# A hand-ordered cross-attention and FFN kernel: the FFN's second half runs one pair later, and the order of every engine is rewritten

## The chip, the cores and the metric

The kernel runs on one core of a Trainium2 chip. The metric is the device time in microseconds (us) from start to end of one launch; three runs of the kernel before gave 957.84, 962.15 and 962.29, median 962.15. The engines are named as in the profile: PE is TensorE (matrix products), PEld its weight loads, DVE is VectorE, ACT is ScalarE, POOL is GpSimd, SP is the engine that issues most DMAs. All of them work through their own list of instructions strictly in order and meet only at semaphores.

## The reference

32 batches of 56 queries attend with 16 heads (head size 8) to 1500 context rows each; then comes a feed-forward net with ternary weights and 8-bit activations.

```
x = x + xattn(layernorm(x), ctx, ctx, mask)      # q,k,v projections with bias, 16 heads,
                                                 # softmax(where(mask==0, -1e9, q.k/sqrt(8))) @ v, Wo, bo
x = x + ffn(layernorm(x))                        # gelu(bitlinear(x,w1)) -> bitlinear(.,w2)
bitlinear(x,w): round(x*127/max|x|) clipped, times ternary w (by mean |w|)
```

## The kernel before

The 32 batches go through one software pipeline. A step is one batch; steps come in pairs (even, odd), and `steps` runs `first_even`, `first_odd`, then a loop over 14 pairs of `even` and `odd`, then `last_even`, `last_odd`, and at last `tail`. What an engine does in a step is a written list of words, and all engines' lists have to agree on the order in which PSUM banks are filled. The words and what they do:

- `T0..T2` (PE transposes of the context, L741; ACT copies them out to `ctx_t`, L621), `K0..K2` (key projection, L744; ACT writes `k_full` by `kf`, L641, then `k_hi` by `kh`, L651; POOL writes `k_lo` by `kl`, L573), `V0..V2` (value projection, L748; ACT copies, L631). T and K are for the batch two ahead, V for the next.
- `sum` (ACT, L611: whether a query has any key) then `some` (DVE), `F0` (PE, L751; DVE writes `q_flag`), `q` (POOL: `q_hi`, `q_lo`, `qry_hi`, `qry_lo`, L562 to L566).
- `M0..M11` (PE, L803): products of next batch's queries with keys, only for the row maxima. Each is two products of 64 rows and 500 columns, each in a bank of its own; DVE takes each with `m` (L1091). `neg0`, `R0` turn the maxima into `shift`, which a DMA puts into `own_query`.
- `S0..S11` (PE, L820; `s0 f0` is S0 in two parts): this batch's scores, per chunk of 125 keys four products (hi/hi, hi/lo, lo/hi and the mask bias), each as two 64-row products side by side; ACT takes the two banks of a chunk with `e` (L659, exponential).
- `P0..P2` (PE, L856): probabilities times values, in tiles of 32 columns, for four chunks each. `own0`, `D0` (denominators, L772) and `O0` (output projection, L768) follow; O0 is done once for a pair of batches, and DVE adds it to `x_rows` (L1066).
- The output chain of a pair after that: `rows0` (layer norm statistics, 14 dependent small DVE operations from L900 on), `rows1` (normalise and quantise, L952 to L962), `H0` (PE transposes the rows, L777), `G0` (first FFN product, L779; ACT applies gelu, L628), `hid0..hid3` (DVE quantises the hidden layer, L982 to L992), `U0` (PE transposes it, L782), `Y0` (second product, L786; DVE adds to `x_rows`, L1078), and a DMA stores the rows.

M and S products use half of PE's rows each, side by side (64 rows); the others use the full array (P: tiles of 32 columns).

PSUM has one bank for P and seven (`NBANK`) for all else. A slot is a bank's turn; slots go round in PE's written order, S and M taking two each. So a slot can be filled only when the slot seven places earlier has been read out:

```
bank = {s: (n - len(slots)) % NBANK for n, s in enumerate(slots)}
```

`wait_bank_free` makes PE wait for that reader, `wait_bank_full` the reader for PE. The line with `left_bank` says which semaphore a reader moves. ACT holds one function table at a time: gelu needs another than exp, and a load of a table stands in its list where a function is not in the present one.

Of the kernel before, what the change touches and what calls it, by code (L numbers as in the profile page):

```python
# [126 lines left out]
def passes(open_, lead, even, odd, tail, more_even, more_odd):  # L127

    return {"open": order(open_), "lead": order(lead), "first_even": with_more(even, more_even, ahead=(0, 1, 2)),
            "first_odd": with_more(odd, more_odd), "even": even, "odd": odd,  # L130
            "last_even": ahead_only(even, (-1, 0, 1)), "last_odd": ahead_only(odd, (-1, 0)), "tail": order(tail)}
# [1048 lines left out]
```

How the kernel before makes its waits and increments, by code:

```python
        def wait(e, semaphore, value):  # L360
            if not isinstance(value, int) or value > 0:
                e.wait_ge(semaphore, value)
# [28 lines left out]
        def wait_bank_free(e, slot, how, st):  # L392
            last, ago = before(how, slot)
            if last is not None:
                e.wait_ge(left_bank[last[0]], number(last, later(st, -ago)))
# [1 line left out]
        def wait_bank_full(e, slot, how, st):  # L397
            k = BANK[how][slot]
            e.wait_ge(bank_full[k], fills_before(how, st[1], k) + signalled(how, k).index(slot) + 1)
# [34 lines left out]
            def place_shift(bt):  # L434
                b, k, p = bt
                sp.wait_ge(shift_ready, b + 1)
                for h in range(2):
                    row = SLOT * h + SQ
                    sp.dma_start(own_query[row:row + 1, p, :, :].bitcast(F32),
                                 shift[4 * h:4 * (h + 1), :, 0:SQ].bitcast(F32)).then_inc(shift_placed[p], 16)
# [1 line left out]
            def store(bt):  # L443
                t, rows = pair_of(bt), PAIR * D
                at, added = t * rows, t + 1
                if not isinstance(t, int):
                    at, added = sp.snap(at), sp.snap(added)
                sp.wait_ge(out_ready, added)
                src = x_flat[:, bass.ds(t * D if isinstance(t, int) else sp.snap(t * D), D)]
                sp.dma_start(out_flat[bass.ds(at, rows)].rearrange("(r d) -> r d", d=D), src).then_inc(stored, 16)
# [124 lines left out]
            def fold_bias():  # L576
                pool.wait_ge(xn_ready, NGRP)
                pool.wait_ge(bo_folded, 1)
```

## Time and profile before

| | |
|---|---|
| runs | 957.84, 962.15, 962.29 us |
| the profiled execution | 959.75 us, span from first to last instruction 958.0 us |
| PE busy | 887.8 us, 93% of the span |
| DVE busy | 753.1 us, 79% |
| ACT busy | 673.4 us, 70% |
| POOL busy | 231.5 us, 24% |
| mean granted PE clock | 0.976 of full |
| one loop iteration (two batches) | 54.17 us |

A busy share is an average over the span; PE's ends are modelled, so that two products that overlap in the pipeline both count. The distance between the starts of two products is the better measure of what PE pays. A row of a timeline has the start in us, its length, the engine, the line, the operation, what it writes and reads, how many instructions are merged, and in brackets the idle time ahead of it with what ended it.

### The profile page before, as it was taken

To read this page: it belongs to the slowest core of one execution; us is meant where nothing else is said; L and a number is where in the kernel's file an instruction comes from. 1 tells how busy PE (TensorE), PEld (TensorE's weight loads), DVE (VectorE), ACT (ScalarE), POOL (GpSimd) and SP (SyncE) were. 2 spreads that over 40 slices of the span, in tenths; PEclk is the share of its full clock that TensorE was granted. 3 is DMA by queue.
4 is the path that set the end of the run, shared out by engine and by line. 5 is a ranking of instruction groups with operands and counts; after the bars stand their busy time and mean duration, and the time that the engine had idled before them with its cause. 6 is when DMAs were issued, how large, how long until landed. Compare 5 with 4: busy or idle time off the path is not lost.

```text
span 958.0 us, 33628 instructions
## 1 busy us (share of the span) xinstructions
PE 887.8 (93%) x11716; PEld 694.2 (72%) x11716; DVE 753.1 (79%) x2593; ACT 673.4 (70%) x1272; POOL 231.5 (24%) x253
## 2 busy tenths in 40 slices
PE   3767989999999999999999999999999999999983
PEld 2344767777787787778787777777787777778772
DVE  3687568888788878888788888888787888888744
ACT  2543667777887877777886777777887777777661
POOL 6310142230222222130222222131222222031200
PEclk9788999999999999999999999999999999999997
DMA  5520221122222211122222211122222111220000
GB/s 130 127 62 1 63 61 29 42 57 60 63 60 63 59 34 47 46 60 60 63 60 63 53 32 50 51 60 60 63 60 61 49 32 50 56 60 0 4 2 6
DMA packets 59375, 49.34 MB, mean 52 GB/s; under 512 B 2785, under 2 KB 55633, under 8 KB 59345
## 3 DMA queue, kind: packets, MB, share of 16 engines
q1 hardware_dynamic: 57551, 48.11, 19.0%
q10 hardware_dynamic: 1793, 0.83, 0.4%
q8 instruction: 18, 0.29, 0.1%
q14 instruction: 13, 0.10, 0.0%
HBM read 47.91 MB, written 0.92 MB: 51 GB/s over the span
## 4 chain that ended last, share of the span: by engine, by line
issue 66%; POOL 18%; PE 7%; DVE 5%; ACT 1%; DMA 1%; POOLq 1%; DVEq 0%; ACTq 0%
POOL k_lo L573 8%; POOL qry_hi L565 4%; POOL qry_lo L566 4%; PE ps_p L820 2%; DMA ctx_sb<-in_ctx_dram 1%; PE ps_p L803 1%; DVE max_junk L1091 1%; POOL q_lo L563 1%; POOL q_hi L562 1%; PE ps_v L856 1%; PE ps_p L744 1%; ACT probs L659 1%; POOL x_rows L581 0%; PE ps_p L741 0%; POOLq L556 0%
## 5 line engine op out<-in xcount | busy, mean ns | idle before, releaser
L1091 DVE CUSTOM_DVE_ANT_0 max_junk<-ps_p,mask_bias 120x500 bf16<-120x500 f32 x768 | 481.6, 675 | 125.3 <-PE ps_p L803 104.5
L659 ACT ACTIVATE probs<-ps_p 125x448 f32<-125x448 f32 x768 | 359.3, 551 | 87.0 <-PE ps_p L820 81.6
L573 POOL TENSOR_TENSOR k_lo<-k_full,k_hi 128x500 fp32r<-128x500 f32 x96 | 119.8, 1262 | 592.0 <-ACT k_hi L651 587.2
L856 PE MATMUL ps_v<-probs,vals 125*32 125x112 f32 x6144 | 162.9, 262 | 0.8 <-issue 0.4
L803 PE MATMUL ps_p<-k_hi,qry_hi 64*120 64x500 f32 x768 | 148.8, 413 | 15.6 <-POOL qry_hi L565 6.5
L820 PE MATMUL ps_p<-qry_hi,k_hi 64*125 64x448 f32 x768 | 158.6, 403 | 4.4 <-DVE seg_max L1091 1.7
L856 PEld LDWEIGHTS ps_v<-probs,vals 125*32 125x32 f32 x6144 | 146.9, 111 | 21.1 <-issue 17.7
L641 ACT ACTIVATE k_full<-ps_p,bk_sb 128x500 f32<-128x500 f32 x96 | 64.7, 674 | 123.1 <-PE ps_p L744 122.6
L820 PE MATMUL ps_p<-own_query,mask_bias 57*125 57x448 f32 x768 | 145.7, 368 | 0.0
L820 PE MATMUL ps_p<-qry_lo,k_hi 64*125 64x448 f32 x768 | 144.4, 366 | 0.0
L820 PE MATMUL ps_p<-qry_hi,k_lo 64*125 64x448 f32 x768 | 144.3, 365 | 0.0
L803 PEld LDWEIGHTS ps_p<-k_hi,qry_hi 64*120 64x120 f32 x768 | 71.5, 181 | 51.7 <-issue 22.4
L820 PEld LDWEIGHTS ps_p<-qry_hi,k_hi 64*125 64x125 f32 x768 | 74.7, 185 | 47.0 <-ACT probs L659 17.4
L744 PE MATMUL ps_p<-ctx_t,wk_sb 128*128 128x500 f32 x192 | 100.8, 620 | 4.1 <-DVE seg_max L1091 4.0
L748 PE MATMUL ps_p<-wv_sb,ctx_t 128*125 128x128 f32 x768 | 100.9, 278 | 0.7 <-DVE seg_max L1091 0.7
L748 PEld LDWEIGHTS ps_p<-wv_sb,ctx_t 128*125 128x125 f32 x768 | 90.1, 188 | 10.3 <-issue 9.0
L820 PEld LDWEIGHTS ps_p<-own_query,mask_bias 57*125 57x125 f32 x768 | 75.0, 184 | 5.2 <-DMA own_query<-shift 0.4
L820 PEld LDWEIGHTS ps_p<-qry_lo,k_hi 64*125 64x125 f32 x768 | 74.9, 185 | 5.2
L820 PEld LDWEIGHTS ps_p<-qry_hi,k_lo 64*125 64x125 f32 x768 | 75.4, 186 | 4.1
L741 PE MATMUL ps_p<-ident,ctx_sb 125*128 125x125 f32 x384 | 57.7, 282 | 13.8 <-DMA ctx_sb<-in_ctx_dram 13.8
L631 ACT ACTIVATE vals<-ps_p 125x512 f32<-125x512 f32 x96 | 55.6, 597 | 18.8 <-PE ps_p L748 17.1
L1091 DVE DVE_READ_ACCUMULATOR2_ANT seg_max<- 120x1 f32 x768 | 63.8, 83 | 0.0
(124 smaller groups left out, 831.5 us busy)
## 6 DMA issues: line engine op xcount, KB each, us to landing
ctx_sb<-in_ctx_dram SPq DMA_DIRECT2D x31, 750.0 KB
mask_sb<-in_mask_Bx1xSxS_ik_dram SPq DMA_DIRECT2D x64, 328.1 KB
own_query<-shift SPq DMA_DIRECT2D x64, 1.8 KB
out_dram<-x_rows SPq DMA_DIRECT2D x16, 56.0 KB, 1.6
ctx_sb<-in_ctx_dram ACTq DMA_DIRECT2D x1, 750.0 KB
x_rows<-in_x_dram SPq DMA_DIRECT2D x1, 672.0 KB, 10.9
w_sb<-in_L_ffn_w_dram SPq DMA_DIRECT2D x2, 256.0 KB, 8.8
x_rows<-in_x_dram SPq DMA_DIRECT2D x1, 224.0 KB, 5.9
```

The source lines that it names most:

```text
L565: put_q(pool.tensor_tensor(qry_hi[:, p, :, 0:SQ], head_of_row[:], heads_of(q_hi[:]), ALU.mult))
L573: pool.tensor_tensor(k_lo[:, p, at], k_full[:, (p + n) % 2, :], k_hi[:, p, at].bitcast(F32), ALU.subtract)\
L631: act.activation(vals[:, p, 4 * n:4 * n + 4, :, 0, :].rearrange("p c v r -> p (c v) r"), bank[0:KC, :].rearrange("p (v r) -> p v r", r=VH) ...
L641: act.activation(k_full[:, (p + n) % 2, :], ps_p[:, BANK[how]["K", n, 0], 0:SEG], ACT.Identity, bias=bk_sb[:, 0:1]).then_inc(k_full_ready, 1)
L659: act.activation(probs[:, c % NP, h], ps_p[0:KC, BANK[how]["S", c, h], 0:HC], ACT.Exp)\
L741: mm = pe.transpose(bank[:, c * KC:(c + 1) * KC], ctx_sb[:, p, 4 * n + c, :], ident[0:KC, 0:KC])
L744: mm = pe.matmul(bank[:, 0:SEG], wk_sb[:], ctx_t[:, p, n * SEG:(n + 1) * SEG], start=True, stop=True)
L748: mm = pe.matmul(bank[0:KC, c * D:(c + 1) * D], ctx_t[:, p, at:at + KC], wv_sb[:], start=True, stop=True)
L803: pe.matmul(ps_p[0:MROWS, BANK[how]["M", n, h], 0:SEG], qry_hi[rows, p, 2 * r:2 * r + 2, :].rearrange("p a q -> p (a q)")[:, 0:MROWS], k_h ...
L820: mm = pe.matmul(ps_p[0:KC, BANK[how]["S", c, h], 0:HC].rearrange("k (a q) -> k a q", a=HH), key[part, :], query[part], start=(n == 0), st ...
L856: mm = pe.matmul(ps_v[r:r + VT, col:col + PAIR], vals[:, p, c, t].rearrange("p a r -> p (a r)"), src, start=(c == 0 and t < 4), stop=(c == ...
L1091: dve.tensor_tensor_reduce(max_junk[0:MROWS, BANK[how][slot], :], ps_p[0:MROWS, BANK[how][slot], 0:SEG], mask_bias[0:MROWS, p, s * SEG:(s ...
```

## The change

`U`, `Y` and `hid` get a lag of two pairs instead of one (`PAIR_LAG`): a pair's `rows`, `H0`, `G0` still run in the same pair of steps, while `hid0..hid3`, `U0` and `Y0` run in the even step after. Since the second pair of steps has no such work yet, it becomes a variant of its own (`early_even`, `early_odd`), the loop has 13 iterations instead of 14, and the one tail becomes three (`tail_even`, `tail_odd`, `tail_last`), with one more store at the end.

```
+PAIR_LAG = {"U": 2, "Y": 2, "hid": 2}
...
-        def pair_of(st):
-            return st[1] - 1
+        def pair_of(st, kind=""):
+            return st[1] - PAIR_LAG.get(kind, 1)
...
-            with e.Fori(1, B // 2 - 1) as i:
+            step(batch(1, 0), "early_even")
+            step(batch(1, 1), "early_odd")
+            with e.Fori(2, B // 2 - 1) as i:
...
-    PE_EVEN, PE_ODD, "D0 O0 H0 G0 U0 Y0",
+    PE_EVEN, PE_ODD, ("D0 U0 O0 Y0", "H0 G0", "U0 Y0"),
...
-    DVE_EVEN, DVE_ODD, "own D0 O0 rows0 rows1 H0 hid0 hid1 hid2 hid3 U0 Y0",
+    DVE_EVEN, DVE_ODD, ("hid0 own D0 hid1 hid2 hid3 U0 O0 rows0 rows1 Y0", "H0", "hid0 hid1 hid2 hid3 U0 Y0"),
...
-                if p == 1 and (loop or b > 1):
+                if p == 1 and (loop or b > 3):
                     store(bt)
...
+            store(batch(B // 2 + 1, 1))
```

All lists of the two loop steps are new. In PE's, the stretches of full-array words between M and S words become fewer and longer; the four even and odd lists of PE and ACT are:

```
before, PE even: T0 T1 V0 M0 s0 f0 M1 S1 S2 M2 S3 M3 S4 S5 M4 S6 S7 M5 M6 P0 D0 K0 M7 S8 S9 M8 S10 M9 O0 S11 M10 M11
                 T2 K1 F0 V1 V2 K2 R0 P1 P2
before, PE odd:  V0 T0 H0 s0 M0 f0 S1 S2 M1 S3 S4 M2 M3 G0 P0 M4 S5 M5 S6 S7 M6 S8 S9 M7 S10 S11 M8 M9 P1 P2 M10 M11
                 K0 U0 V1 T1 Y0 T2 D0 K1 F0 K2 R0 V2
after, PE even:  T0 V0 K0 T1 M0 s0 f0 S1 M1 S2 M2 S3 S4 M3 S5 M4 S6 S7 M5 S8 M6 M7 P0 P1 M8 S9 M9 S10 S11 M10 M11
                 D0 V1 U0 T2 V2 F0 K1 O0 P2 K2 Y0 R0
after, PE odd:   T0 V0 T1 T2 K0 H0 M0 s0 f0 M1 S1 S2 M2 S3 S4 M3 S5 S6 M4 S7 S8 M5 S9 M6 S10 S11 M7 M8
                 K1 V1 V2 K2 G0 M9 M10 M11 P0 P1 P2 F0 R0 D0
before, ACT odd: sum0 V0 T0 e0 ... e9 G0 e10 ... e23 kf0 kh0 T1 V1 T2 kf1 kh1 kf2 V2 kh2
after, ACT odd:  T0 V0 T1 T2 kf0 e0 ... e21 kh0 e22 e23 kf1 V1 V2 kf2 sum0 kh1 kh2 G0
```

On ACT, the head of the even step in the kernel before (`ctx_t` is a T word, `vals` a V word, `probs` an exponential; ISA and REGISTER_ALU rows are waits and their registers):

```order
L621 ACTIVATE ctx_t<-ps_p 128x500
L399 ISA
L621 ACTIVATE ctx_t<-ps_p 128x500
L363 ISA
L631 ACTIVATE vals<-ps_p 125x32x16
L363 ISA
L658 ISA
L659 ACTIVATE probs<-ps_p 125x448 x2
L658 REGISTER_ALU
L659 ACTIVATE probs<-ps_p 125x448 x2
```

The same place on ACT in the changed kernel, behind the first `ctx_t` (`mask_sum_junk` is the word `sum0`, `k_full` is `kf0`); the row that follows is the first exponential:

```order
L623 ACTIVATE mask_sum_junk,mask_sum<-mask_sb 56x1500
L406 ISA
L370 ISA
L653 ACTIVATE k_full<-ps_p,bk_sb 128x500
L406 ISA
L370 ISA
L643 ACTIVATE vals<-ps_p 125x32x16
L406 ISA
L633 ACTIVATE ctx_t<-ps_p 128x500
L370 ISA
L670 ISA
L671 ACT_TABLE_LOAD
```

The mask sum and `k_full` have moved ahead of the first exponential, and the load of the exp table, which stood behind gelu in the middle of the odd step's exponentials, now stands between the last copy and the first exponential of the even step.

On PE, the way from the even step's `R0` to the odd step's `H0` (`w_sb` into `ident_bf`, 128x112) in the kernel before:

```order
L753 MATMUL ps_p<-ident,neg_max 8x120
L856 MATMUL ps_v<-probs,vals 32x112 x32
L850 ISA
L856 MATMUL ps_v<-probs,vals 32x112 x32
L748 MATMUL ps_p<-wv_sb,ctx_t 125x128 x4
L741 MATMUL ps_p<-ident,ctx_sb 128x125 x4
L777 MATMUL ps_p<-ident_bf,w_sb 128x112
```

And in the changed kernel from the second row behind O0 (`wo_rows,attn`) on, which now stands in this same stretch, to H0:

```order
L870 MATMUL ps_v<-probs,vals 32x112 x32
L747 REGISTER_ALU
L758 MATMUL ps_p<-ctx_t,wk_sb 128x500
L800 MATMUL ps_p<-w2t,w_sb 112x128 x4
L767 MATMUL ps_p<-ident,neg_max 8x120
L755 MATMUL ps_p<-ident,ctx_sb 128x125 x4
L762 MATMUL ps_p<-wv_sb,ctx_t 125x128 x4
L755 MATMUL ps_p<-ident,ctx_sb 128x125 x8
L747 ISA
L758 MATMUL ps_p<-ctx_t,wk_sb 128x500
L791 MATMUL ps_p<-ident_bf,w_sb 128x112
```

O0 stood between M and S words before, with two S and M words, nine full-array words and both P words between it and H0; now P2, K2, Y0, R0 and five T, V, K words lie between.

## Rows read from the trace of the kernel before

**Rows 1.** One loop iteration; busy us and instructions by engine, then clock, DMA:
```profile
400.77:454.94 54.17, 53.48 (x733) 42.34 (x732) 45.06 (x156) 41.77 (x80) 13.24 (x15) 1.00 0.20 54
```
**Rows 2.** Timeline of PE, even step, second half:
```profile
421.28 0.40 PE L803 MATMUL ps_p<-k_hi,qry_hi 64*120 64x500 f32 x2
421.61 0.69 PE L768 MATMUL ps_p<-wo_rows,attn 128*112 128x128 f32 x4
422.23 0.47 PE L820 MATMUL ps_p<-qry_hi,k_hi 64*125 64x448 f32 x2
422.53 0.36 PE L820 MATMUL ps_p<-qry_hi,k_lo 64*125 64x448 f32 x2
...
423.15 0.61 PE L803 MATMUL ps_p<-k_hi,qry_hi 64*120 64x500 f32 x4
423.70 0.65 PE L741 MATMUL ps_p<-ident,ctx_sb 125*128 125x125 f32 x4
424.18 1.01 PE L744 MATMUL ps_p<-ctx_t,wk_sb 128*128 128x500 f32 x2
...
425.05 1.99 PE L748 MATMUL ps_p<-wv_sb,ctx_t 128*125 128x128 f32 x16
426.88 1.00 PE L744 MATMUL ps_p<-ctx_t,wk_sb 128*128 128x500 f32 x2
...
427.92 3.27 PE L856 MATMUL ps_v<-probs,vals 125*32 125x112 f32 x128
...
432.97 0.22 PE L777 MATMUL ps_p<-ident_bf,w_sb 112*128 112x112 bf16 x1 [0.28 <-DVE w_sb L962]
```
**Rows 3.** Timeline of PE, even step's M0:
```profile
406.56 0.48 PE L803 MATMUL ps_p<-k_hi,qry_hi 64*120 64x500 f32 x2 [0.25 <-issue]
```
**Rows 4.** Timeline of ACT, the even step's end and the odd step:
```profile
429.96 1.45 ACT L611 ACTIVATE mask_sum_junk<-mask_sb 56x1500 bf16<-56x1500 int32 x1
...
432.37 0.60 ACT L631 ACTIVATE vals<-ps_p 125x512 f32<-125x512 f32 x1 [0.88 <-PE ps_p L748]
432.87 0.58 ACT L621 ACTIVATE ctx_t<-ps_p 128x500 f32<-128x500 f32 x1
...
440.55 0.69 ACT L628 ACTIVATE wtern<-ps_p,row_stat 112x512 f32<-112x512 f32 x1
441.26 1.28 ACT L659 ACT_TABLE_LOAD   x1
442.55 6.49 ACT L659 ACTIVATE probs<-ps_p 125x448 f32<-125x448 f32 x14
```
**Rows 5.** The page's groups, ACT's k_full:
```profile
L641 ACT ACTIVATE k_full<-ps_p,bk_sb 128x500 f32<-128x500 f32 x96 | 64.7, 674 | 123.1 <-PE ps_p L744 122.6
```
**Rows 6.** Timeline of PE in the odd step, scores beside gelu:
```profile
442.71 0.36 PE L820 MATMUL ps_p<-own_query,mask_bias 57*125 57x448 f32 x2
443.15 0.47 PE L820 MATMUL ps_p<-qry_hi,k_hi 64*125 64x448 f32 x2
```
**Rows 7.** Timeline of DVE, from O0's sum to rows1's last:
```profile
423.06 0.29 DVE L1066 TENSOR_TENSOR x_rows<-ps_p,x_rows 112x128 f32 x1
...
426.55 0.28 DVE L900 BATCH_NORM_STATS2 row_stat<-x_rows 112x6 f32 x1
...
430.28 1.03 DVE L952 TENSOR_SCALAR w_sb<-x_rows,row_stat 112x128 f32 x1
...
432.68 0.23 DVE L962 TENSOR_SCALAR w_sb<-w_sb 112x128 bf16<-112x128 f32 x1
```
**Rows 8.** Timeline of POOL, first odd step:
```profile
126.21 4.71 POOL L581 TENSOR_TENSOR x_rows<-x_rows,bo_sb 112x2048 f32<-112x2048 f32 x1
```
**Rows 9.** Timeline of PE, the loop's first M0:
```profile
133.21 0.48 PE L803 MATMUL ps_p<-k_hi,qry_hi 64*120 64x500 f32 x2 [2.88 <-POOL qry_hi L565]
```
**Rows 10.** A window behind that wait, columns as in rows 1:
```profile
134.70:138.10 3.40, 3.40 (x20) 2.99 (x20) 1.67 (x6) 2.05 (x5) 1.97 (x2) 0.50 0.62 166
```
**Rows 11.** Timeline of PE, H0 of the last pair of steps:
```profile
918.96 0.22 PE L777 MATMUL ps_p<-ident_bf,w_sb 112*128 112x112 bf16 x1 [1.93 <-DVE w_sb L962]
```

More of the change, by code:

```diff
@@ L64 @@
 PE_EVEN = order("""
-    T0 T1 V0 M0 s0 f0 M1 S1 S2 M2 S3 M3 S4 S5 M4 S6 S7 M5 M6 P0 D0 K0 M7 S8 S9 M8 S10 M9 O0 S11 M10 M11 T2 K1 F0
-    V1 V2 K2 R0 P1 P2
+    T0 V0 K0 T1 M0 s0 f0 S1 M1 S2 M2 S3 S4 M3 S5 M4 S6 S7 M5 S8 M6 M7 P0 P1 M8 S9 M9 S10 S11 M10 M11 D0 V1 U0 T2
+    V2 F0 K1 O0 P2 K2 Y0 R0
 """)
 ACT_EVEN = order("""
-    T0 T1 V0 e0 e1 e2 e3 e4 e5 e6 e7 e8 e9 e10 e11 e12 e13 e14 e15 sum0 kf0 e16 e17 e18 e19 e20 e21 e22 kh0 e23
-    T2 kf1 kh1 kf2 V1 V2 kh2
+    T0 sum0 kf0 V0 T1 e0 e1 e2 e3 e4 e5 e6 e7 e8 e9 e10 e11 e12 e13 e14 e15 e16 e17 e18 e19 e20 e21 e22 e23 kh0
+    kf1 T2 V1 V2 kh1 kf2 kh2
 """)
 DVE_EVEN = order("""
-    own0 m0 m1 m2 m3 m4 m5 m6 m7 m8 m9 bias0 m10 m11 m12 m13 D0 m14 m15 m16 m17 m18 m19 O0 some0 bias1 m20 m21
-    m22 m23 F0 neg0 rows0 R0 rows1 bias2
+    own0 hid0 m0 m1 m2 m3 m4 m5 hid1 m6 m7 m8 m9 some0 m10 hid2 m11 m12 m13 m14 bias0 hid3 m15 m16 m17 m18 m19
+    m20 m21 m22 m23 D0 U0 O0 neg0 F0 rows0 Y0 R0 rows1 bias1 bias2
 """)
@@ L87 @@
 PE_ODD = order("""
-    V0 T0 H0 s0 M0 f0 S1 S2 M1 S3 S4 M2 M3 G0 P0 M4 S5 M5 S6 S7 M6 S8 S9 M7 S10 S11 M8 M9 P1 P2 M10 M11 K0 U0 V1
-    T1 Y0 T2 D0 K1 F0 K2 R0 V2
+    T0 V0 T1 T2 K0 H0 M0 s0 f0 M1 S1 S2 M2 S3 S4 M3 S5 S6 M4 S7 S8 M5 S9 M6 S10 S11 M7 M8 K1 V1 V2 K2 G0 M9 M10
+    M11 P0 P1 P2 F0 R0 D0
 """)
 ACT_ODD = order("""
-    sum0 V0 T0 e0 e1 e2 e3 e4 e5 e6 e7 e8 e9 G0 e10 e11 e12 e13 e14 e15 e16 e17 e18 e19 e20 e21 e22 e23 kf0 kh0
-    T1 V1 T2 kf1 kh1 kf2 V2 kh2
+    T0 V0 T1 T2 kf0 e0 e1 e2 e3 e4 e5 e6 e7 e8 e9 e10 e11 e12 e13 e14 e15 e16 e17 e18 e19 e20 e21 kh0 e22 e23
+    kf1 V1 V2 kf2 sum0 kh1 kh2 G0
 """)
 DVE_ODD = order("""
-    H0 own0 m0 m1 m2 m3 m4 m5 m6 m7 m8 m9 m10 m11 hid0 m12 m13 bias0 m14 m15 hid1 m16 some0 hid2 hid3 m17 bias1
-    m18 m19 m20 m21 U0 m22 m23 neg0 Y0 bias2 D0 R0 F0
+    H0 m0 m1 m2 m3 m4 m5 m6 m7 m8 m9 bias0 m10 m11 m12 m13 m14 m15 own0 m16 m17 m18 m19 m20 some0 m21 m22 m23
+    neg0 bias1 R0 F0 D0 bias2
 """)
 POOL_ODD = order("""
-    kl0 q0 kl1 kl2
+    kl0 kl1 kl2 q0
 """)
@@ L129, in passes @@
     return {"open": order(open_), "lead": order(lead), "first_even": with_more(even, more_even, ahead=(0, 1, 2)),
[L130 to L131 removed]
+            "first_odd": with_more(odd, more_odd), "early_even": [s for s in even if s[0] not in PAIR_LAG],
+            "early_odd": odd, "even": even, "odd": odd,
+            "last_even": ahead_only(even, (-1, 0, 1)), "last_odd": ahead_only(odd, (-1, 0)),
+            "tail_even": order(tail[0]), "tail_odd": order(tail[1]), "tail_last": order(tail[2])}
 PE_PASS = passes(
@@ L182, in fills_before @@
 def fills_before(how, i, bank):
-    first = sum(len(signalled(h, bank)) for h in ("open", "lead", "first_even", "first_odd"))
+    first = sum(len(signalled(h, bank)) for h in ORDER[:ORDER.index(None)])
     body = len(signalled("even", bank)) + len(signalled("odd", bank))
     if how in ("even", "odd"):
-        return first + (i - 1) * body + (len(signalled("even", bank)) if how == "odd" else 0)
-    order = ["open", "lead", "first_even", "first_odd", None, "last_even", "last_odd", "tail"]
-    return sum((B // 2 - 2) * body if h is None else len(signalled(h, bank)) for h in order[:order.index(how)])
+        return first + (i - 2) * body + (len(signalled("even", bank)) if how == "odd" else 0)
+    return sum((B // 2 - 3) * body if h is None else len(signalled(h, bank)) for h in ORDER[:ORDER.index(how)])
 def before(how, slot):
@@ L199, in before @@
         return None, 0
-    there = PREVIOUS[how]
-    return [s for s in FLAT[there] if BANK[there][s] == bank][-1], 1
+    there, ago = PREVIOUS[how], 1
+    while not any(BANK[there][s] == bank for s in FLAT[there]):
+        there, ago = PREVIOUS[there], ago + 1
+    return [s for s in FLAT[there] if BANK[there][s] == bank][-1], ago
 def xattn_ffn(nc, x, ctx_in, mask, wq, bq, wk, bk, wv, bv, wo, bo, w1, w2, out):
```

37 lines of the change are left out of this document (24 added, 13 removed).

## The prediction

> **What bounds the kernel now.** I read the page's shares first, then the windows of single loop iterations, then PE's timeline through one iteration, and last the timelines of ACT and DVE at the places where PE's products are further apart than usual. An iteration (one pair of batches) takes 54.17 us, and PE is busy for 53.48 of it at full clock, with DVE at 45.06 and ACT at 41.77 [rows 1]. So PE is the path, and the sum is made on PE: what it pays for crossing between kinds of product, and where it waits in its written order. The chain of waits is of little use here (it follows POOL); distances between the starts of PE's products tell more.
>
> A crossing is seen in rows 2. Two maxima pairs and the way out of them to T0 take 0.55 us (423.15 to 423.70), one pair and the way out to O0 0.33 (421.28 to 421.61): so a pair costs 0.22 and the way out 0.11. Behind O0 the first score product holds PE for 0.30 (422.23 to 422.53), where the ones after it are some 0.20 apart: 0.1 for coming back, beside a way out of O0 that I price like the way in, 0.11. That is the price that the change attacks.
>
> **Crossings.** I count in the two lists. Before, an iteration has six stretches of full-array words between M and S words, which makes 12 crossings, and inside them 4 more between P (tiles of 32 columns) and full-array words; after, four stretches with 8, and 3 inside. 5 crossings fewer by 0.11 are 0.55 us, and two returns to M and S fewer by 0.1 are 0.2: -0.75 us an iteration. Bounds: 0 if crossings hide behind weight loads in the new places, -1.5 if each costs twice as much. I take -0.75, since rows 2 show it at two places.
> The Trainium skill has a rule for this (TensorEngine Tiling (Array Packing), Key Properties: a change of tiling mode drains TensorE, a change of tile alone does not). The trace agrees that something of this kind is paid, with 0.11 us a time; by that rule alone the kernel would get faster, which is the first rival below.
>
> **Waits that go.** M0 of the even step waits 0.25 us before and starts with a refill [rows 3]; it is held by POOL's qry_hi, which needs F0. In the new lists F0 stands ahead of R0, D0, T0, V0, K0, T1, some 3 us before M0 and about as long as the chain of q_flag, q_hi, q_lo and qry_hi; -0.3. Gelu with its two table loads no longer stands among the odd step's exponentials: there a score product came 0.44 behind its forerunner instead of 0.20 and the next paid the refill [rows 6]; -0.35.
>
> **The head of the even step: a wait that comes.** This is the largest term. ACT's list there is now T0, sum0, kf0, V0, T1, table load, e0. Let PE start T0 at 0. T0's copy can start at about 0.75 (0.65 of products [rows 2] and a hand-over of 0.1) and the next ACT instruction 0.5 later (432.37 to 432.87 [rows 4]), at 1.25. The mask sum takes 1.45 and a little for reading the sum: 2.8. k_full 0.67 [rows 5]: 3.45. V0 0.5: 3.95. T1 0.58: 4.55. The table load is 1.28, and no gap stands on either side of it (gelu ends at 441.24, load 441.26 to 442.54, exponential 442.55 [rows 4]): 5.83. e0, 0.55, ends at 6.4.
> PE in the same time: T0 0.48, V0 0.91, K0 0.84, T1 0.48 [rows 2] make 2.7; M0 with its way in 0.33, S0 0.9, S1 0.8, M1 0.2: it wants S2 at 4.95. But S2 takes the slots seven behind M0's second and S0's first, so it waits for e0, until about 6.45: 1.5 us. It restarts with a refill of 0.1. The exponentials then come 0.46 apart (6.49 less 0.55, by 13 [rows 4]); S3 needs e3, at 7.8, where PE would be ready at 7.5: 0.3 more. After that ACT has caught up, because two scores and a maximum (1.85 on PE) give it as long as its four exponentials need. Together +1.95 us. ACT reaches this place in time otherwise: in the odd step's end P0, P1, P2 give it 4.8 us (1.6 each by 3.27 for two [rows 2]) for sum0, kh1, kh2, the gelu table and gelu, so F0, which needs gelu's bank, does not wait. Bounds: 0 (if S2 is not held) and +2.6 (if ACT comes 0.6 late).
> On the table the Trainium skill says more than the trace (ScalarE: Activation LUTs, What ACT_TABLE_LOAD costs: 1283 ns for the load and some 1380 ns of drain at every switch). By that page the term would be an estimated 1.4 us larger in each of 13 iterations, 18 us in all. The trace agrees on the load and shows no drain (0.02 us on one side, 0.01 on the other [rows 4]), so the sum goes without it.
>
> **H0: a wait that grows.** Before, O0 stood in the even step's S and M words; DVE had its sum at 423.06, and H0 still waited for rows1 to end [rows 2, 7]. The bracket says 0.28, from T0's start I make it 0.44. Now O0 stands behind K1, and the chain from O0 to H0 is shorter on PE than on DVE. DVE: O0's products and hand-over 0.75, its sum 0.3, neg0 and F0 0.2, from the first of rows0 to rows1's first 3.73 [rows 7] with the 0.23 of waiting in it out and Y0's sum (0.27) in: 3.77; rows1 from 430.28 to 432.91, 2.63; 0.05 to PE. That is 7.7. PE from O0: O0 0.55, P2 1.65, K2 0.95, Y0 and R0 0.35, T, T, T 1.35, V0 0.9, K0 0.85, in all 6.6. H0 waits 1.1 to 1.2, against 0.44: +0.75. Nothing hides it: behind H0 on PE stand M0 and all scores of the odd step, and ACT and DVE are idle until then. Bounds: 0 (rows1's first, 1.03 us here, has the shape of operations that take 0.3 us) and +1.3.
>
> **Other edits.** hid0 to hid3 and U0, Y0 are the same work in another step; DVE has 9 us free in an iteration [rows 1], and in the even step they lie beside the new wait of S2: nothing. The store waits for a Y0 that is now done a step earlier: nothing, and place_shift, behind it in SP's queue, is not held. q0 behind kl1 and kl2 on POOL: both end before q_flag is there.
>
> **Once only.** At the first loop iteration PE waits 2.88 us for POOL [rows 9], because bias folding (4.71 us [rows 8]) stands between kl0 and q0 and kl0 came late; 1.5 us after it the granted clock is 0.50, 1.2 GHz, for 3.4 us [rows 10], in which half, 1.7, is lost. In the new list kh0 comes before e22, so kl0 and the folding start earlier and run beside P0 to P2: -4.6. Bounds 0 and -4.6. The last pair and the tail: H0 waits 1.93 already [rows 11] and will wait some 1.5 more, gelu no longer splits the last scores (-1.5), and the tail has one more hid and U0 ahead of O0 (+1.5 to +3): together +1, bounds -2 and +5. The second pair has no table load at its head; I count it as 0.
>
> **The sum.** -0.75 - 0.3 - 0.35 + 1.95 + 0.75 = +1.3 us an iteration, by 13 iterations +17; -4.6 + 1 for what is once only: +13.3. The profiled execution took 959.75 (span 958.0): 973. The median of the runs is 962.15, 2.4 above it, so between 973 and 975.5; I say 974, 1.2% slower.
>
> **Rivals.**
> Fewer crossings win (ends on the other side). If PE's S2 is not held at the even head (ACT arrives at e0 before PE has S0 and M1 behind it) and H0's wait stays as it was, then -1.4 by 13, -4.6, +1: about 938. It decides as soon as the head's wait is under 0.65 with H0's +0.75, or under 1.4 without it. For: crossings and the M0 wait are plain in the rows, and ACT is only 77% busy in an iteration. Against: four ACT operations and a load stand in writing between T0 and e0, and their durations are measured; only PE being later than I think helps. Chance 0.2.
> They cancel. Half the head's wait (0.95) and half of H0's growth (0.4): -0.05 an iteration; with the once-only part 956 to 962. For: both are differences of sums of ten terms each. Chance 0.13.
> The clock falls. The wait of 2.88 was followed by 3.4 us at 1.2 GHz [rows 9, 10]; if the new waits of 1.5 and 1.2 us do the same once in each iteration, 1.7 us by 13 come on top: 996. For: such waits now come in every iteration. Against: they are half as long, with a busy PE on both sides. Chance 0.1.
> The forecast has the remaining 0.57, with a range of its own of 964 to 985.
>
> A difference under 0.5% (about 4.8 us) is what a measurement of this kernel cannot tell from none. Faster by more: the first rival, 0.2. Within: the second, and the forecast's low edge, 0.14. Slower: 0.66. The range, 950 to 990, leaves out the lower part of the first rival and the clock.
>
> **What would show it.** In the changed kernel's PE timeline: a gap of about 1.5 us ahead of the score chunk that follows the even step's M1, ended by ACT's probs; a table load directly ahead of e0, with ACT busy from T0's copy up to it; H0's idle at 1.1 us, released by rows1's last; the iteration's length at 55.5; no wait for POOL at the loop's first M0. Wrong would be: an iteration under 54, or e0 starting less than 0.5 us behind the end of S0.

## The result

The changed kernel takes 980.57 us (median of four runs, 978.93 to 983.31), the kernel before 961.01 in the same session: the ratio is 1.0211, with a 95% interval of 1.0175 to 1.0247. The forecast was 974, slower by 1.2%; it is slower by 2.1%. The profiled execution took 983.31 us, its span 981.6, against 958.0 before: 23.6 us more. The medians differ by 19.6; the profiled execution is the slowest of the changed kernel's four, and its start is part of why (see "Once only").

I put the 23.6 on the places of the trace by the distances between H0 (one in each pair of steps from the second on). The first H0 is at 161.37 before and at 157.57 after: -3.8. From there to that of the last pair of steps (rows 11 before, 942.59 after) are 14 distances, 757.6 us before and 785.0 after: +27.4, or 1.96 each. From that H0 to the end are 39.1 us before and 39.0 after. A loop iteration, which took 54.17 us [rows 1], now takes 56.16. A window of one iteration of the changed kernel: us, then busy us and instructions of PE, PEld, DVE, ACT and POOL, then clock and DMA:

```profile
494.70:550.86 56.16, 53.76 (x730) 42.66 (x731) 46.80 (x156) 41.78 (x79) 13.28 (x14) 1.00 0.19 52
```

PE has nearly the same busy time (53.48 before) at full clock; 1.7 of the 2 us are idle time. PE's timeline shows two places where most of it lies. The even step's head (answers to rows 3):

```profile
517.12 0.20 PE L765 MATMUL ps_p<-some_diag,ones_bf 128*128 128x56 bf16 x1
517.29 0.26 PE L767 MATMUL ps_p<-ident,neg_max 120*8 120x120 f32 x1
517.51 0.47 PE L786 MATMUL ps_p<-pv_own,den_of_row 128*128 128x112 f32 x2
518.10 0.64 PE L755 MATMUL ps_p<-ident,ctx_sb 125*128 125x125 f32 x4
...
520.95 0.49 PE L817 MATMUL ps_p<-k_hi,qry_hi 64*120 64x500 f32 x2
...
522.91 0.39 PE L817 MATMUL ps_p<-k_hi,qry_hi 64*120 64x500 f32 x2
524.26 0.47 PE L834 MATMUL ps_p<-qry_hi,k_hi 64*125 64x448 f32 x2 [0.96 <-ACT probs L671]
...
525.18 0.45 PE L817 MATMUL ps_p<-k_hi,qry_hi 64*120 64x500 f32 x2
525.65 0.47 PE L834 MATMUL ps_p<-qry_hi,k_hi 64*125 64x448 f32 x2
```

M0 (520.95) no longer waits. Behind M1 (522.91) the chunk S2 starts 1.35 us later, where a maxima pair needs 0.20; behind M2 the chunk S3 starts 0.47 later. ACT in the same stretch (answers to rows 4):

```profile
514.29 1.28 ACT L640 ACT_TABLE_LOAD   x1
515.58 0.69 ACT L640 ACTIVATE wtern<-ps_p,row_stat 112x512 f32<-112x512 f32 x1
518.78 0.59 ACT L633 ACTIVATE ctx_t<-ps_p 128x500 f32<-128x500 f32 x1 [2.50 <-PE ps_p L755]
519.26 1.44 ACT L623 ACTIVATE mask_sum_junk<-mask_sb 56x1500 bf16<-56x1500 int32 x1
520.60 0.19 ACT L623 ACTIVATION_READ_ACCUMULATOR mask_sum_junk<-mask_sb 56x1 f32 x1
520.71 0.68 ACT L653 ACTIVATE k_full<-ps_p,bk_sb 128x500 f32<-128x500 f32 x1
521.29 0.59 ACT L643 ACTIVATE vals<-ps_p 125x512 f32<-125x512 f32 x1
521.76 0.59 ACT L633 ACTIVATE ctx_t<-ps_p 128x500 f32<-128x500 f32 x1
522.37 1.28 ACT L671 ACT_TABLE_LOAD   x1
523.67 2.73 ACT L671 ACTIVATE probs<-ps_p 125x448 f32<-125x448 f32 x6
```

From T0's copy (518.78) to the first exponential ACT has no pause; before that it stands idle for 2.50 us with gelu's table in it. The forecast had put S2 at 6.45 us behind T0's start; it is 6.16 (518.10 to 524.26).

The second place is H0, first on PE (answers to the end of rows 2), then the chain on DVE (answers to rows 7):

```profile
542.97 0.66 PE L782 MATMUL ps_p<-wo_rows,attn 128*112 128x128 f32 x4
...
548.66 1.01 PE L758 MATMUL ps_p<-ctx_t,wk_sb 128*128 128x500 f32 x2
550.86 0.22 PE L791 MATMUL ps_p<-ident_bf,w_sb 112*128 112x112 bf16 x1 [1.19 <-DVE w_sb L978]
```

```profile
543.78 0.29 DVE L1082 TENSOR_TENSOR x_rows<-ps_p,x_rows 112x128 f32 x1 [0.66 <-PE ps_p L782]
...
548.37 0.83 DVE L968 TENSOR_SCALAR w_sb<-x_rows,row_stat 112x128 f32 x1
...
550.58 0.23 DVE L978 TENSOR_SCALAR w_sb<-w_sb 112x128 bf16<-112x128 f32 x1
```

From O0's start to H0's are 7.89 us, set by O0's products and DVE's chain behind them; the forecast had 7.7.

**Where an iteration's time goes.** For each word of PE I take the distance to the next word's start, less what such a word takes where nothing is in its way (a maxima pair 0.20, a transpose 0.11 and so on). What is left over in an iteration, mean of six iterations, in us:

| | before | after | difference | forecast |
|---|---|---|---|---|
| ways between M/S, full-array and P words (16, then 11) | 1.97 | 1.54 | -0.43 | -0.55 |
| the refill behind such a way | 1.15 | 0.89 | -0.26 | -0.20 |
| M0's wait | 0.30 | 0 | -0.30 | -0.30 |
| gelu's table among the scores | 0.34 | 0 | -0.34 | -0.35 |
| head of the even step (M1 to S2, M2 to S3, two refills) | 0 | 1.61 | +1.61 | +1.95 |
| H0 | 0.45 | 1.34 | +0.89 | +0.75 |
| small waits inside M/S stretches | 1.20 | 1.52 | +0.32 | 0 |
| small waits inside full-array stretches | 0.25 | 0.71 | +0.46 | 0 |
| in none of these lines | 0 | 0.04 | +0.04 | 0 |
| sum | 5.66 | 7.65 | +1.99 | +1.30 |

### The profile page after: what moved, and what is told of

Read it like the earlier page. It is cut to its first block, busy times and chain, and to the rows that moved or that the text cites. A ratio compares the mean times of both kernels' runs of the same rounds, so it can differ in the third digit from the quotient of the medians.

```text
span 981.6 us, 33626 instructions
## 1 busy us (share of the span) xinstructions
PE 890.9 (91%) x11716; PEld 700.3 (71%) x11716; DVE 776.2 (79%) x2593; ACT 670.4 (68%) x1270; POOL 232.2 (24%) x253
## 4 chain that ended last, share of the span: by engine, by line
issue 60%; POOL 16%; PE 15%; DVE 6%; DMA 1%; ACT 1%; POOLq 1%; DVEq 0%; ACTq 0%
POOL k_lo L585 8%; PE ps_p L834 6%; POOL qry_hi L577 3%; POOL qry_lo L578 3%; PE ps_v L870 2%; PE ps_p L817 2%; PE ps_p L758 1%; DMA ctx_sb<-in_ctx_dram 1%; DVE max_junk L1107 1%; PE ps_p L762 1%; POOL q_lo L575 1%; POOL q_hi L574 1%; PE ps_p L755 1%; POOLq L568 0%; DVE ps_p L1068 0%
## 5 line engine op out<-in xcount | busy, mean ns | idle before, releaser
L834 PE MATMUL ps_p<-qry_hi,k_hi 64*125 64x448 f32 x768 | 156.3, 395 | 13.4 <-ACT probs L671 12.7
L817 PE MATMUL ps_p<-k_hi,qry_hi 64*120 64x500 f32 x768 | 157.9, 424 | 9.3 <-DVE seg_max L1107 4.5
L870 PE MATMUL ps_v<-probs,vals 125*32 125x112 f32 x6144 | 158.0, 260 | 0.4 <-issue 0.2
L758 PE MATMUL ps_p<-ctx_t,wk_sb 128*128 128x500 f32 x192 | 104.7, 630 | 2.6 <-DVE seg_max L1107 2.6
L762 PEld LDWEIGHTS ps_p<-wv_sb,ctx_t 128*125 128x125 f32 x768 | 92.1, 190 | 9.2 <-ACT probs L671 7.6
L633 ACT ACTIVATE ctx_t<-ps_p 128x500 f32<-128x500 f32 x96 | 54.1, 584 | 45.6 <-PE ps_p L755 45.6
```

Source lines behind the costliest of these rows:

```text
L633: act.activation(ctx_t[:, p, n * SEG:(n + 1) * SEG], bank[:, 0:SEG], ACT.Copy)\
L758: mm = pe.matmul(bank[:, 0:SEG], wk_sb[:], ctx_t[:, p, n * SEG:(n + 1) * SEG], start=True, stop=True)
L762: mm = pe.matmul(bank[0:KC, c * D:(c + 1) * D], ctx_t[:, p, at:at + KC], wv_sb[:], start=True, stop=True)
L817: pe.matmul(ps_p[0:MROWS, BANK[how]["M", n, h], 0:SEG], qry_hi[rows, p, 2 * r:2 * r + 2, :].rearrange("p a q -> p (a q)")[:, 0:MROWS], k_h ...
L834: mm = pe.matmul(ps_p[0:KC, BANK[how]["S", c, h], 0:HC].rearrange("k (a q) -> k a q", a=HH), key[part, :], query[part], start=(n == 0), st ...
L870: mm = pe.matmul(ps_v[r:r + VT, col:col + PAIR], vals[:, p, c, t].rearrange("p a r -> p (a r)"), src, start=(c == 0 and t < 4), stop=(c == ...
```

## The experiments

The length of an iteration (mean of nine) is the measure; it is free of what differs at the start from run to run. The changed kernel has 56.16, before 54.17. A time without a ratio is that of a single run.

**The table load ahead of its wait.** A one-column exponential behind gelu brings exp's table back at once:

```
                     act.activation(... gelu ...)
+                    wait(act, table_back, pair_of(st))
+                    act.activation(table_junk[:], bk_sb[:], ACT.Exp).then_inc(table_back, 1)
```

> The changed kernel with one more tiny exponential (128x1, into a scratch tile) right behind gelu on ACT, so that the exp table is loaded there, in ACT's 2.5 us of idle time ahead of T0, and not ahead of e0. Theory: e0 starts 1.3 us earlier, the gap M1 to S2 shrinks from 1.35 us to some 0.3, M2 to S3 from 0.47 to 0.22: -1.4 us an iteration, 14 times, about 961 to 963. Rival (the mask sum and k_full hold ACT anyway): under -0.5 an iteration, above 973.

Measured: 965.94, ratio 1.0058 (1.003 to 1.0086), iteration 55.05. That is 1.11 an iteration less, where 1.4 was expected. The leftover at S2 falls from 1.15 to 0.27 and that at S3 disappears. ACT's timeline:

```profile
504.67 0.69 ACT L642 ACTIVATE wtern<-ps_p,row_stat 112x512 f32<-112x512 f32 x1
505.37 1.28 ACT L644 ACT_TABLE_LOAD   x1
506.67 0.20 ACT L644 ACTIVATE table_junk<-bk_sb 128x1 f32<-128x1 f32 x1
507.85 0.59 ACT L635 ACTIVATE ctx_t<-ps_p 128x500 f32<-128x500 f32 x1 [0.98 <-PE ps_p L759]
```

The load now stands in what was ACT's idle time. This is the cause of 1.1 of the 1.6 us at the head. The Trainium skill (ScalarE: Activation LUTs, What ACT_TABLE_LOAD costs) counts 1283 ns of load and about 1380 ns of drain at a switch. The load of 1.28 us is here; no drain shows at either load, also not between two of them (0.01 to 0.02 us around each).

**The mask sum out of the head.** `sum0` moves behind e17, DVE's `some0` behind m15:

```
-    T0 sum0 kf0 V0 T1 e0 ... e17 e18
+    T0 kf0 V0 T1 e0 ... e17 sum0 e18
```

> The changed kernel with ACT's mask sum of the even step moved from between T0 and kf0 to behind e17, where ACT is idle while PE does P0 and P1 (and DVE's some0 moved behind m15). My theory of the head wait: the load of the exp table stands behind the wait for the first scores, so ACT's queue ends at T1 (522.35 in the changed kernel's trace), hardly later than S0 does (about 522.3), and the load of 1.28 follows either way. So the sum is hidden and this gives only 0 to -0.1 us an iteration: 978 to 982. Rival (the sum as the cause, as the prediction added it up): e0 comes 1.5 us earlier, the wait at S2 of 1.15 goes, with its refills 1.6 us an iteration, 22 us over 14: about 958.

Measured: 987.95, ratio 1.0279 (1.0244 to 1.0314), iteration 56.70. The expected time was 978 to 982. The leftover at S2 is unchanged, 1.17: so not the sum of ACT's work holds S2, but the load, which stands behind e0's wait for S0 and can't start earlier. I had not said this in the forecast, where sum and load were terms of one chain. The time got worse because `some0` now waits for the late sum and holds up maxima behind it. PE's timeline:

```profile
537.61 0.38 PE L817 MATMUL ps_p<-k_hi,qry_hi 64*120 64x500 f32 x2
538.46 0.47 PE L834 MATMUL ps_p<-qry_hi,k_hi 64*125 64x448 f32 x2 [0.46 <-DVE seg_max L1107]
```

**O0 earlier.** PE: D0 behind P1, O0 behind M11; DVE: D0 behind m15, O0 behind m23.

```
-    ... P0 P1 M8 S9 ... M11 D0 V1 U0 T2 V2 F0 K1 O0 P2
+    ... P0 P1 D0 M8 S9 ... M11 O0 V1 U0 T2 V2 F0 K1 P2
```

> The changed kernel with D0 of the even step right behind P1 and O0 right behind M11 on PE, DVE's D0 behind m15 and its O0 behind m23. Theory: H0 waits because the DVE chain from O0's products to rows1's end takes 7.9 us (542.97 to 550.86) against 6.6 on PE; with the chain started 1.8 us earlier H0's wait (1.34 by distances) falls to 0.0 to 0.2: -1.2 us an iteration, about 964 to 967. Rival (PE then waits elsewhere, since DVE is simply behind in this stretch): the maxima after H0 or the scores behind them wait instead, above 975.

Measured: 975.62, ratio 1.0148 (1.0106 to 1.019), iteration 55.69. The rival held (PE waits elsewhere, above 975). H0 doesn't wait any more (leftover 0.10, 1.24 less), but 0.72 of that come back at S10, which needs the bank of m16, and DVE does D0 (1.2 us) ahead of m16:

```profile
533.01 0.39 PE L817 MATMUL ps_p<-k_hi,qry_hi 64*120 64x500 f32 x2
534.06 0.47 PE L834 MATMUL ps_p<-qry_hi,k_hi 64*125 64x448 f32 x2 [0.66 <-DVE seg_max L1107]
```

**All three.**

```
 ACT table early; ACT sum0 behind e17; PE and DVE D0, O0 earlier, as above
```

> The three edits of e1, e2 and e3 together. If the head wait and H0's wait are what the changed kernel lost, it takes 56.15 - 1.5 - 1.2 = 53.4 us an iteration against 54.17 before, and 981.6 - 14 x 2.7 = 944 in all, faster than both kernels. If DVE and bank limits take the place of these waits, an iteration stays at 54.2 or more and the time at 955 or more.

Measured: 965.96, ratio 1.0039 (1.0015 to 1.0064), iteration 54.99, no better than the first edit alone. S2's leftover is 0.34, H0's 0.11, but S10's is now 1.18: two of the edits hold up the same maxima on DVE. The expectation added gains of edits that collide at one place.

**The hidden layer in the odd step.** hid0 to hid3, U0 and Y0 go to the odd step, still a pair late; then the same with the early table and the early O0.

```
-PE even: ... D0 V1 U0 T2 V2 F0 K1 O0 P2 K2 Y0 R0
+PE even: ... D0 V1 T2 V2 F0 K1 O0 P2 K2 R0
-PE odd:  ... M8 K1 V1 V2 K2 G0 ...
+PE odd:  ... M8 K1 U0 V1 V2 Y0 K2 G0 ...
```

> The changed kernel with hid0 to hid3, U0 and Y0 moved from the even to the odd step, still one pair late and ahead of G0 (DVE: hid0 behind m3, hid1 behind m7, hid2 behind m11, hid3 behind m15, U0 and Y0 behind own0; PE: U0 behind K1, Y0 behind V2). Theory: the lag put 2.8 us of DVE work into the even step, where DVE is behind, so that PE's waits for banks in its scores and maxima (0.4 to 0.5 us an iteration) and Y0's place in the chain to H0 (0.3) come from it; the head wait stays. -0.7 us an iteration, 970 to 974. Rival (the waits in the even step come from the density of maxima there, and the odd step then gets the same waits): within 2 us of the changed kernel.

> e5 with the exp table loaded behind gelu (e2) and D0, O0 early (e3). If the waits are independent once DVE has room in the even step, 56.15 - 0.7 - 1.1 - 1.2 = 53.2 us an iteration and about 941 in all, faster than the kernel before. If DVE's D0 still holds up the bank of S10 as in e3 and e4 (0.8 to 1.2 us), it is 54.2 and 955.

Measured: 1025.49, ratio 1.0666 (1.0625 to 1.0707), iteration 59.53; and 985.15, ratio 1.0249 (1.0205 to 1.0293), iteration 56.51. Both expectations missed, the first by 50 us. Two words more in the odd step shift its ring of banks. That a slot takes the bank of the slot seven places earlier holds within a step; `banks` counts back from the end of each list, and so where a list has no multiple of seven slots its first words have nearer neighbours. With 62 slots in the changed kernel's odd step T0 takes F0's bank, six places earlier; with 64 it takes R0's, the slot just ahead, and DVE reads R0's only behind the 14 operations of `rows0`. PE's timeline:

```profile
568.28 0.27 PE L767 MATMUL ps_p<-ident,neg_max 120*8 120x120 f32 x1
570.58 0.62 PE L755 MATMUL ps_p<-ident,ctx_sb 125*128 125x125 f32 x4 [2.03 <-DVE shift L1044]
```

From R0's start to T0's are 2.30 us instead of 0.11: 2.2 us are the price of one neighbour in the ring. It hides H0's wait (1.35 less between K0 and H0). Of the rest, DVE's added work in the odd step makes waits at M7, M8 and U0 of 0.3 to 0.5 each, and some 0.75 of the 3.4 us is PE's clock: in six of the 13 iterations the granted clock is 0.50 (1.2 GHz) for 3.4 us from 1.2 us behind that wait on. Five of them take 60.4 to 60.5 us and the loop's first 61.2, the others 58.8 or less. Such a window, in the iteration that starts at 421.1:

```profile
452.60:456.00 3.40, 3.40 (x13) 2.38 (x12) 1.76 (x8) 1.81 (x4) 0.80 (x1) 0.50 0.16 46
```

The second variant, where the way from R0 to T0 is 0.95, has no such window in its loop. What the moved work alone costs, with good neighbours, stays open.

**Two crossings more.** M9 moves between V1 and V2 in the odd step:

```
-    K1 V1 V2 K2 G0 M9 M10 M11 P0
+    K1 V1 M9 V2 K2 G0 M10 M11 P0
```

> The changed kernel with one word moved: M9 of the odd step from behind G0 to between V1 and V2, which makes two more crossings between full-array and 64-row products and nothing else. Theory: 0.12 into M9 and 0.1 out of it, perhaps 0.1 for the refill behind: +0.2 to +0.35 us an iteration (from the distances of H0 in the trace). Rival (crossings cost nothing of their own, the gaps are waits for banks): 0.

Measured: 978.13 in one run, iteration 55.72: shorter by 0.44, where the theory had it longer and the rival unchanged. PE's timeline:

```profile
507.21 1.04 PE L762 MATMUL ps_p<-wv_sb,ctx_t 128*125 128x128 f32 x8
508.17 0.49 PE L817 MATMUL ps_p<-k_hi,qry_hi 64*120 64x500 f32 x2
508.59 1.14 PE L762 MATMUL ps_p<-wv_sb,ctx_t 128*125 128x128 f32 x8
```

The way into M9 costs 0.09 over V1's 0.87, the way out 0.21 (0.42 less 0.20), the refill behind it 0.10: 0.41 together, as expected and a little more. But the small waits inside full-array stretches fell from 0.71 to 0.26 (D0 to T0 0.24 and F0 to R0 0.13 are gone), one way from M11 to P0 became 0.10 cheaper, and the refills inside those stretches went with them. Around S2 the total stayed (1.15, now in two parts), and so did H0's.

The gain lies at the odd step's end: the distances F0 to R0, R0 to D0 and D0 to T0 are 0.17, 0.22 and 0.59 in the changed kernel and 0.04, 0.10 and 0.26 here, together 0.58 less. R0 transposes `neg_max`, which DVE makes behind its last maximum. In the changed kernel DVE and POOL do this, and R0 starts at 517.29 (timelines of DVE and of POOL):

```profile
513.90 1.26 DVE L1029 TENSOR_SCALAR some_diag<-ident,some_key 56x56 bf16<-56x56 f32 x1
...
516.98 0.18 DVE L1116 TENSOR_REDUCE neg_max<-seg_max 120x8 f32<-120x24 f32 x1
```

```profile
513.84 2.51 POOL L585 TENSOR_TENSOR k_lo<-k_full,k_hi 128x500 fp32r<-128x500 f32 x2 [4.76 <-ACT k_hi L663]
```

With M9 moved they do this, and R0 starts at 516.14:

```profile
512.93 0.24 DVE L1029 TENSOR_SCALAR some_diag<-ident,some_key 56x56 bf16<-56x56 f32 x1
...
515.10 0.18 DVE L1116 TENSOR_REDUCE neg_max<-seg_max 120x8 f32<-120x24 f32 x1
```

```profile
513.30 2.49 POOL L585 TENSOR_TENSOR k_lo<-k_full,k_hi 128x500 fp32r<-128x500 f32 x2 [5.38 <-ACT k_hi L663]
```

`some_diag` takes 1.26 us where it starts 0.06 behind POOL's `k_lo` and 0.24 where it is through before it. The 1.02 us put `neg_max` so late that R0 starts 0.13 behind its end; with M9 moved 0.86 lie between them. T0, the first word behind the loop's jump, comes late with R0: in all runs of variants in which R0 waits so, T0 starts 0.59 to 0.61 behind D0, in the others 0.25 to 0.34. R0's bank neighbour isn't the reason, since DVE had read that bank (M9's) ahead of `some_diag`. No run moved `some_diag` alone; the cause is read from these rows, which are alike in every iteration. So a crossing has its price, and the gain of this edit came from elsewhere.

**DVE out of the way.** Each maximum over 250 columns instead of 500, which leaves out half of every maximum, in the changed kernel and in the kernel before:

```
-    dve.tensor_tensor_reduce(max_junk[0:MROWS, BANK[how][slot], :], ps_p[..., 0:SEG], ...
+    dve.tensor_tensor_reduce(max_junk[0:MROWS, BANK[how][slot], 0:SEG // 2], ps_p[..., 0:SEG // 2], ...
```

> The changed kernel with each of DVE's 768 maxima over 250 instead of 500 columns, which leaves out half of the maximum. DVE is far from busy then. Theory: the head wait (ACT) stays at 1.15 + 0.27, the small bank waits and H0's wait in part go (the chain from O0 to H0 starts earlier by what DVE's D0 is late): 55.2 to 55.5 us an iteration. Rival (DVE sets the pace, the head wait is a symptom): the head wait shrinks too, under 54.5.

> The kernel before, with each DVE maximum taken over 250 of its 500 columns (leaves out half of each maximum). With the same cut in the changed kernel the iteration went from 56.15 to 55.23 us: 0.93 of it had been PE waiting for banks that DVE reads late. Theory: the changed lists made DVE the second bound (longer runs of maxima, DVE words put on the way), and before had little of it: its iteration goes from 54.17 only to 53.9 or so (0.2 to 0.4 less), and the difference between the two kernels with the cut is 1.2 to 1.4: head, H0, M0 and table swap alone. Rival: before has the same bank waits and loses them as well, to 53.2; then the waits aren't of the change.

Measured: iteration 55.23 (964.34) in the changed kernel, 53.21 (940.36) in the kernel before. The first was as expected, the second was not: the rival has it, and DVE's speed was worth as much before. Before loses 0.96 us by the cut, after 0.93, and the difference between them is 2.02, as without it. So DVE's speed doesn't explain the 2 us. Where the 0.96 go differs: before it is H0's wait (0.45) and some small ones; after, H0's 1.34 stay to a hundredth, since its chain has no maximum in it, and all 0.93 are small waits, 0.50 of them at the odd step's end, where `some_diag` takes 0.24 again (F0 to R0, R0 to D0, D0 to T0: 0.04, 0.10, 0.34). In the table's last two lines of waits the growth is 0.78 with full maxima and 0.47 with halves: a part of the small waits is DVE's, the other stays open.

**Towards a better version.** First the early table and M9 ahead of V2 together, then O0's chain as well, moved this time by a word or two where DVE bounds it:

```
-PE even:  M11 D0 V1 U0 T2 V2 F0 K1 O0 P2        DVE even: m20 m21 m22 m23 D0 U0 O0 neg0
+PE even:  M11 D0 V1 T2 V2 O0 U0 F0 K1 P2        DVE even: m20 m21 D0 m22 m23 O0 U0 neg0
```

> The changed kernel with two edits: an exponential of one column behind gelu, which brings the table load to the odd step's end, and M9 ahead of V2. Theory: the head's wait (worth 1.11 us an iteration alone) and the bank neighbours (0.44 alone) are at different places and add: iteration 54.6, total near 960. Rival: both take from the same waits (M9's move had shortened the head's wait from 1.15 to 0.89): 55.0, total 965 to 966, as the first edit alone.

> The same two edits, and O0's chain moved up where DVE bounds it: DVE does D0 ahead of the last two maxima, PE does O0 behind V2 and ahead of U0, F0, K1, and DVE takes O0 before U0. Theory: DVE has O0's sum 1.0 us earlier, U0 costs 0.25 of it, PE waits some 0.4 for the bank of the last maximum but no longer at H0 (1.34 now): iteration 53.9, total 950 to 953, below the kernel before. Rival: DVE's D0 (1.1 us) ahead of maxima only moves the wait, as it did ahead of m16: 54.5 and 959 to 962.

Measured: 967.46, ratio 1.006 (1.0036 to 1.0085), iteration 55.03: nothing over the table alone, so the rival held: the full-array waits are gone as before, but S2's leftover is 0.49 instead of 0.27 and the way there 0.24 longer. And 959.15, ratio 0.9972 (0.9949 to 0.9996), iteration 54.30, where theory had 53.9 and the rival 54.5. PE's timeline of the latter:

```profile
538.73 1.01 PE L762 MATMUL ps_p<-ctx_t,wk_sb 128*128 128x500 f32 x2
539.57 0.21 PE L795 MATMUL ps_p<-ident_bf,w_sb 112*128 112x112 bf16 x1
```

H0 follows K0 without a wait; of the 1.34 some 0.4 came back ahead of F0 (its bank is that of the last maximum) and 0.2 behind P2.

**The mask sum once more.** In the last kernel: `sum0` behind e17 with `some0` behind m19 this time, and at the even step's end V1, T2, V2 ahead of `kf1` on ACT:

```
-    T0 sum0 kf0 V0 T1 e0 ... e17 e18 ... kh0 kf1 T2 V1 V2 kh1
+    T0 kf0 V0 T1 e0 ... e17 sum0 e18 ... kh0 V1 T2 V2 kf1 kh1
```

> The last combination (table load early, M9 ahead of V2, O0's chain moved up; iteration 54.30) with two more edits of order: the even step's mask sum behind e17, where ACT idles 4.1 us while PE does P0 and P1, with its DVE word behind m19; and at the even step's end ACT takes V1, T2, V2 ahead of k_full, for which it idled 3.7 us. Theory: ACT was busy without a pause from the odd step's end to e0, so 1.44 us less there ends what is left of the head's wait (0.25, 0.49 and 0.20 in excess), and K2's bank wait (0.34 behind P2) goes: iteration 53.1 to 53.5, total 941 to 948, 1.3 to 2% below the kernel before. Rival: with the head gone DVE or the banks are late at the next chunks (as when all waits were attacked at once): 54.0, 955.

Measured: 955.95, ratio 0.9942 (0.9918 to 0.9965), iteration 54.23; the fastest of all kernels with all of their work, but nearer to the rival (54.0, 955) than to the theory: of the two waits that were to go K2's went, S2's stayed at 0.49. PE's row says ACT; DVE's rows tell who it is. S2 takes the bank of M0's second maximum, and DVE reads that until 510.25:

```profile
510.40 0.47 PE L838 MATMUL ps_p<-qry_hi,k_hi 64*125 64x448 f32 x2 [0.21 <-ACT probs L675]
```

```profile
507.89 0.68 DVE L1002 TENSOR_REDUCE hid_stat<-wtern 112x1 f32<-112x512 f32 x1
508.97 0.68 DVE L1111 CUSTOM_DVE_ANT_0 max_junk<-ps_p,mask_bias 120x500 bf16<-120x500 f32 x1 [0.40 <-DVE hid_stat L1002]
509.58 0.67 DVE L1111 CUSTOM_DVE_ANT_0 max_junk<-ps_p,mask_bias 120x500 bf16<-120x500 f32 x1
```

hid0, which the change has put at the even step's front, stands ahead of both. In the changed kernel DVE reads that bank until 523.24, a microsecond ahead of S2 (524.26): behind ACT's load this second wait was hidden.

## Why the prediction was right, and where a size was off

**The sign and the main terms hold.** The head's wait is where the forecast had it, with the releaser, the ACT list without a pause and the table load that it named; it is 1.61 instead of 1.95, since ACT starts e0 at 523.67, 5.57 behind T0, and the forecast had 5.83. That 1.1 of it are the load's is shown (early table); that the mask sum adds to it was argued and fell: while the load is there, moving the sum leaves S2 as it is. H0's wait is 0.89 more instead of 0.75, for the reason given: the chain from O0 over DVE is 7.89 long, and with O0 earlier the wait is gone. M0's wait and gelu's table among the scores went, at the price written down.

**Crossings.** -0.69 in the table against -0.75. The count (16 to 11) was right, and the price per way nearly (0.12 before, 0.14 after, where 0.11 was forecast). The Trainium skill's sentence (TensorEngine Tiling (Array Packing), Key Properties) that a change of mode drains TensorE agrees with a leftover at every one of them, from 0.09 to 0.21 by the neighbours.

**The step that failed: "Other edits ... nothing".** The forecast held the moved words to be free because DVE had 9 us to spare in an iteration. That is a mean over an iteration and says nothing of one place in it; the small waits grew by 0.78 an iteration, 10 us in 13. Of these 0.46 lie inside full-array stretches, about as much as went with M9's move. Their place is the odd step's end, where R0 waits for DVE's `neg_max`, because the new lists put DVE's `some_diag` beside POOL's `k_lo` and it takes 1.26 us instead of 0.24 (it is 0.24 in every step of the kernel before); that is read from the rows, no run changed it alone. Where it is alone again this place gives back 0.58 (M9 moved) and 0.50 (halved maxima), its refills with it. The number of crossings is not behind it, since M9's move makes two more. The 0.32 inside M/S stretches, which have become longer and have other words seven slots ahead, are not traced to a reader. This term, with the head 0.34 too large, H0 0.14 too small, the crossings 0.06 too large and 0.05 of gelu's table and of what stands in no line, makes 1.99 out of 1.30.

**Once only.** The M0 that was the loop's first (now that of `early_even`) has no wait any more [rows 9], and the 3.4 us from it on run at full clock [rows 10]. The window of the changed kernel, and one behind the H0 of the last pair, which the next paragraphs use:

```profile
129.00:132.40 3.40, 3.40 (x32) 2.65 (x30) 2.62 (x9) 3.40 (x8) 0.99 (x1) 1.00 0.29 87
942.90:946.30 3.40, 3.40 (x20) 3.40 (x22) 0.75 (x3) 1.10 (x3) 0.00 (x0) 0.50 0.07 17
```

The start is 3.8 us shorter, against 4.6. This can't be read finely: among the variants, whose starts are nearly alike, the first H0 lies between 152.49 and 159.56. That of the early table, whose program is the same up to there, has it at 153.55: PE's clock was at half rate for 10.2 us at a stretch near the start there (27.3 to 37.5), and for 20.5 in this execution (24.7 to 45.2). The H0 of the last pair waits 2.1 more [rows 11]; that is part of the 14 distances, and from there to the end the difference is 0; the forecast had +1 for both:

```profile
942.59 0.22 PE L791 MATMUL ps_p<-ident_bf,w_sb 112*128 112x112 bf16 x1 [4.04 <-DVE w_sb L978]
```

**Rivals.** That fewer crossings win, or cancel, fell with the head's wait. That the clock falls is refuted for this kernel: with a wait of 1.0 and one of 1.2 us in each iteration the granted clock is 1.00 over the whole of one, and at half rate only ahead of 99.8, for 3.4 us from 942.9 on, behind H0's wait of 4.04, and in the tail from 963.4 on. The hidden layer in the odd step shows that the rival was near: with a wait of 2.03 in each iteration the clock fell in six of 13, and each fall cost the 1.7 us that the rival had priced.

## What to carry to other kernels

An order by hand in a ring of buffers has two costs per word: its own, and whose buffer it inherits; after every reordering list the pairs "filled here, read there" before counting crossings or busy shares, across the ends of the lists too. Look also at what other engines do beside a moved word: here a DVE operation that met one of POOL's cost 0.58 us an iteration with not one word of PE's in the wrong place. The table load in front of an instruction that waits for data was hidden only when something harmless of the same table stood ahead of the wait. Gains at different waits add only while their edits don't put work ahead of the same reader; here one edit of 1.1 us an iteration and one of 0.5, with a third, made 1.2.
